# A decoder layer on one core: cross-attention fed by large transfers, with one software-pipelined stream

## The reference

```python
x = x + attn(layernorm(x), ...)                 # linear attention, no softmax
# cross-attention, 16 heads of 8, expanded to 16 features per head
f(t) = concat([exp(t @ fm_w.T + fm_b), exp(-(t @ fm_w.T + fm_b))])   # per head
q = f(layernorm(x)); k = f(ctx); v = f(ctx)
scores = einsum('nqhd,nkhd->nhqk', q, k) / sqrt(128)
out = einsum('nhql,nlhd->nqhd', softmax(scores), v)
x = x + out.reshape(N, S, 256) @ fc_w.T + fc_b
x = x + ffn(layernorm(x), ...)                  # top-1 of 16 experts + a shared expert
```

## Time and profile before

| | |
|---|---|
| median of 3 runs | 655.98 us (653.83 to 665.1) |
| the profiled execution | 653.2 us, of which the span from first to last instruction is 651.4 us |
| PE busy | 464.6 us, 71% of the span, mean granted clock 0.866 |
| DVE, ACT, POOL busy | 341.8, 253.6, 190.8 us |
| phase 3: first score product to last residual addition | 199.8 to 424.5 us |

### The profile page before, as it was taken

The page is one execution under the profiler, slowest core; times in us unless marked ns, Lnnn a source line. Parts: engine busy times, 40 slices in busy tenths (PEclk is TensorE's granted clock), DMA queues, the critical chain, the costliest instruction groups (busy, mean ns, idle before and its releaser), DMA issues.

```text
span 651.4 us, 11782 instructions
## 1 busy us (share of the span) xinstructions
PE 464.6 (71%) x3778; PEld 316.6 (49%) x3778; DVE 341.8 (52%) x969; ACT 253.6 (39%) x578; POOL 190.8 (29%) x223
## 2 busy tenths in 40 slices
PE   0488898677731298888889888868982198887760
PEld 0266566444421166566566665524551155766650
DVE  4577885427686246666665666475820123434343
ACT  0446655377750034444443444536710012323320
POOL 3142231657882000000000000020077400555550
PEclk9999999878885559988985889969997599989995
DMA  5720000016689979999997890000041001566739
GB/s 98 282 95 1 0 0 2 0 42 195 198 144 174 181 89 112 117 105 113 104 112 75 90 97 3 3 1 1 1 145 52 33 0 45 157 194 188 203 95 258
DMA packets 101485, 61.94 MB, mean 95 GB/s; under 512 B 33832, under 2 KB 99656, under 8 KB 101320
## 3 DMA queue, kind: packets, MB, share of 16 engines
q1 hardware_dynamic: 91976, 52.92, 46.7%
q0 software_dynamic: 2560, 5.31, 2.4%
q10 hardware_dynamic: 6912, 3.25, 2.2%
HBM read 40.34 MB, written 20.73 MB: 94 GB/s over the span
## 4 chain that ended last, share of the span: by engine, by line
PE 40%; DVE 15%; SPq 12%; issue 8%; DMA 7%; ACT 7%; another core or an unknown queue 7%; POOL 1%; ACTq 1%; DVEq 0%; POOLq 0%
SPq L473 5%; PE bank L711 4%; PE bank L696 4%; PE bank L1204 3%; DMA kst<-kparts 2%; PE bank L1215 2%; ACT prob L853 2%; PE bank L1214 2%; SPq L629 2%; DMA qst<-mT 2%; PE bank L1263 2%; PE bank L734 2%; PE bank L740 2%; PE bank L666 2%
## 5 line engine op out<-in xcount | busy, mean ns | idle before, releaser
L853 ACT ACTIVATE prob<-bank 77x512 f32<-77x512 f32 x128 | 73.7, 592 | 109.7 <-PE bank L696 109.1
L870 POOL COPY vcur<-vals 77x272 f32 (+1 forms) x32 | 13.2, 416 | 190.5 <-PE bank L711 190.5
L1178 POOL DMA_INDIRECT routed<-t_y,t_no x48 | 45.9, 956 | 75.1 <-DVE t_y L1047 63.9
L778 DVE TENSOR_REDUCE mx<-bank 128x5 f32<-128x385 f32 (+1 forms) x96 | 53.7, 580 | 25.1 <-PE bank L666 23.3
L711 PE MATMUL bank<-prob,vcur 77*17 77x128 f32 x1024 | 57.4, 300 | 12.7 <-ACT prob L853 12.4
L666 PE MATMUL bank<-kst,qst 96*128 96x77 bf16 x512 | 40.7, 224 | 34.2 <-DMA kst<-kparts 28.9
L696 PE MATMUL bank<-qst,kst 99*77 99x128 bf16 x512 | 57.4, 243 | 6.7 <-DMA qst<-mT 6.7
L696 PEld LDWEIGHTS bank<-qst,kst 99*77 99x77 bf16 x512 | 43.8, 132 | 17.1 <-issue 9.4
L825 DVE COPY avs_s<-bank 128x512 f32<-128x512 f32 x32 | 22.1, 692 | 56.7 <-PE bank L711 56.7
L666 PEld LDWEIGHTS bank<-kst,qst 96*128 96x128 bf16 x512 | 31.7, 114 | 37.3 <-DMA kst<-kparts 15.5
L941 DVE TENSOR_TENSOR act<-bank,s_g 128x512 f32<-128x512 f32 x24 | 16.5, 688 | 63.3 <-ACT s_g L1115 49.9
(11 more groups left out here) (178 smaller groups left out, 1071.7 us busy)
## 6 DMA issues: line engine op xcount, KB each, us to landing
qst<-qparts SPq DMA_DIRECT2D x96, 128.0 KB, 5.3
t_w<-in_expert_w SPq DMA_DIRECT2D x48, 192.0 KB
qparts<-qpart SPq DMA_DIRECT2D x16, 384.0 KB, 3.4
kparts<-kpart SPq DMA_DIRECT2D x48, 77.0 KB
kst<-kparts SPq DMA_DIRECT2D x16, 231.0 KB, 7.8
sorted_in<-fill SPq DMA_DIRECT2D x1, 3168.0 KB, 10.4
t_row<-sorted_in ACTq DMA_DIRECT2D x48, 66.0 KB
kst<-kparts SPq DMA_DIRECT2D x16, 154.0 KB, 8.1
```

Of the source, the lines that this page charges most:

```text
L778: v.tensor_reduce(mx[:, n // 3, h0:h1], bank[n % 2][:, 0:(h1 - h0) * KEYS].rearrange("p (h k) -> p h k", k=KEYS), AX.X, ALU.max).then_inc( ...
L853: a.activation(prob[u % 2][:].rearrange("p c t -> p (c t)"), bank[2 + u % 2][0:KEYS], ACT.Exp, scale=SCORE_SCALE).then_inc(s["expd"], 1)
L1178: p.indirect_dma_start(out=routed, out_offset=bass.IndirectOffsetOnAxis(ap=t_no[r][:].bitcast(U32), axis=0), in_=t_y[r][:], in_offset=None ...
```

## The change

- **Layout.** `qparts` and `kparts` are now (group, part, feature, head, token), so that all heads and all tokens of a group lie together in one run for a given part and feature: 16 KB for queries (16 heads x 512 tokens of bf16), 9,856 B for keys. To write so, the feature map's columns are ordered feature outside, head inside; each half of the map holds one sign. A write of parts is one transfer per half for keys too (four a group in place of eight).
- **Loads.** A load is for a group of 4 sequences: `load_q` has three transfers and `load_k` three, and the rows of `qst` and `kst` are numbered with the feature outside and the pairing inside. The pairings that use the same query part are read by one transfer with a repeated source. There are three buffers, each of 4 sequences; the third lies in the arena of phase 2. Groups 0 and 1 are loaded in the middle of phase 2 (from group iterations 2 and 3, and 5 and 6); group 2 after all writes; the others when the buffer's last shifted product is done.
- **One stream.** The steps are written out (no loops in phase 3). The value product stands two sets behind the shifted product (LAG = 2), with three `prob` buffers and two banks for the value sums (4 and 5). `avs` is copied by ACT. Values are read in place, without `vcur`.
- **Shift.** The maxima are negated by the reduction itself. The shift's two transfers are issued by POOL. The bias is added by POOL a sequence at a time.

```diff
-    NBUF = 4
+    NBUF = 3
-        qparts = nc.dram_tensor("qparts", (HEADS, EX, PARTS, TOK), BF16).ap()
-        kparts = nc.dram_tensor("kparts", (PARTS, EX, HEADS, B * KEYS), BF16).ap()
+        qparts = nc.dram_tensor("qparts", (NG, PARTS, EX, HEADS, GT), BF16).ap()
+        kparts = nc.dram_tensor("kparts", (NG, PARTS, EX, HEADS, JK), BF16).ap()
...
+            for g in range(NG):
+                if g < NG - 2:
+                    sp.wait_ge(s["ctxTp"], g + 1)
+                    ctx_load(g + 2, g % 2)
+                if g == 2:
+                    sent(0, 1)
+                    load_q(sp, 0)
+                if g == 3:
+                    load_k(sp, 0)
+                if g == 5:
+                    sent(1, 2)
+                    load_q(sp, 1)
+                if g == 6:
+                    load_k(sp, 1)
+                body(g)
...
                     a.copy(vals[:, bass.ds(g * JP + 2 * jj, 2), :, 0:EX],
-                           bank[5 + jj][0:KEYS].rearrange("p (j h e) -> p j h e", j=2, e=EX)).then_inc(s["v_ready"], 1)
+                           bank[5 + jj][0:KEYS].rearrange("p (j e h) -> p j h e", j=2, e=EX)).then_inc(s["v_ready"], 1)
...
+        def load_q(sp, group):
+            r = group % NBUF
             for at, part, n in Q_RUNS:
-                for i in range(n):
-                    sp.dma_start(qst[r][(at + i) * EX:(at + i + 1) * EX],
-                                 qparts[:, :, part, bass.ds(g * JA * S, JA * S)].rearrange("h e t -> e h t")).then_inc(parts_in[r], 16)
+                same = qparts[group, part].rearrange("e (o h) t -> e o h t", o=1).broadcast_to([EX, n, HEADS, GT])
+                sp.dma_start(qst[r][at * EX:(at + n) * EX], same).then_inc(parts_in[r], 16)
+        def load_k(sp, group):
+            r = group % NBUF
             for at, part, n in K_RUNS:
                 sp.dma_start(kst[r][at * EX:(at + n) * EX],
-                             kparts[part:part + n, :, :, bass.ds(g * JA * KEYS, JA * KEYS)].rearrange("a e h t -> (a e) h t")).then_inc(parts_in[r], 16)
+                             kparts[group, part:part + n].rearrange("a e h t -> e a h t")).then_inc(parts_in[r], 16)
...
         def sp_phase3(sp):
+            all_sent(sp, NG // 2)
+            sp.wait_ge(s["vp"], NG)
+            load_q(sp, 2)
+            load_k(sp, 2)
+            for group in range(3, NG):
+                sp.wait_ge(s["bp"], (group - 2) * (2 * 4 * JA))
+                load_q(sp, group)
+                load_k(sp, group)
...
+            for b in range(JP):
+                for u in range(len(UNITS)):
+                    scores(b, u)
+                if b == 2:
+                    turn_shift(0)
+            for n in range(STEPS):
+                b, u = n // 4, n % 4
+                shifted(n)
+                if n >= LAG:
+                    attend(n - LAG)
+                if u < len(UNITS) and b + JP < B:
+                    scores(b + JP, u)
+                if u == 0 and b % JA == 0 and b // JA + 1 < NA:
+                    turn_shift(b // JA + 1)
+                if u == 1 and b >= 2:
+                    turn_back(b - 2)
+                if u == 2 and b >= 2:
+                    project(b - 2)
+                if u == 3 and b >= 1:
+                    turn_values(b - 1)
...
+        def act_phase3(a):
+            copy_shift(0)
+            for n in range(STEPS):
+                b, u = n // 4, n % 4
+                exponentials(n)
+                if u == 0 and b % JA == 0 and b // JA + 1 < NA:
+                    copy_shift(b // JA + 1)
+                if u == 1 and b >= 1:
+                    copy_values(b - 1)
+                if u == 1 and b >= 2:
+                    copy_back(b - 2)
...
+        def pool_phase3(p):
+            p.wait_ge(s["xn2"], NG)
+            for b in range(JA):
+                add_bias(b)
+            shift(0)
+            all_sent(p, NG // 2)
+            p.wait_ge(s["vp"], NG)
+            p.wait_ge(s["xb2"], JA)
+            p.memset(kst[NBUF - 1][ROWS:SHIFT_ROWS], 1.0).then_inc(s["ones_rows"], 1)
+            p.wait_ge(s["ones_rows"], 1 + NBUF)
+            for g in range(1, NA):
+                shift(g)
                 for j in range(JA):
+                    add_bias(g * JA + j)
```

More of the change, by code:

```diff
@@ new lines, in dve_phase3 @@
+            for b in range(B):
+                for u in range(len(UNITS)):
+                    if b + JP < B:
+                        maxima(b + JP, u)
+                if b >= 2:
+                    add_attention(b - 2)
+                if b >= 1:
+                    divide(b - 1)
+                if b >= 2:
+                    statistics(b - 2)
+                if b % JA == JA - 1 and b + JP < B:
+                    parts((b + JP) // JA)
+            add_attention(B - 2)
+            divide(B - 1)
@@ L1335, in _ @@
             sp_fill(sp)
-            sp_phase2(sp, lambda g: load_parts(sp, g, g))
+            sp_phase2(sp)
             sp_phase3(sp)
```

417 lines of the change are left out of this document (174 added, 243 removed).

## The result

The changed kernel takes 681.04 us (median of 4 runs, 676.52 to 684.50), the kernel before 655.84 us on the same chip (4 runs, 653.83 to 665.10). The ratio is 1.039, 95% interval 1.030 to 1.048: slower, where 8% faster was forecast. The profiled execution took 683.24 us, 30.0 more than that of before, with a granted clock of 0.79 against 0.87. Executions of one kernel scatter by some per cent, and a ratio with an interval leaves out those that were more than 1.5% above the kernel's shortest.

The account below looks back on a forecast made before the run. The prediction took phase 3 as bounded by its stream's start, a PE-bound sequence with some waiting, and the tail. Stream start 206.5 + 165 = 371 us, 53 us sooner, so 653.2 - 53 = 600 us; range 576 to 628.

Parts of the forecast that it names:

- part 5: Clock in the attention: half clock only at the start and one short stretch, 24 us, three sequences of 8.0 us.
- the sum: Phase 3's stream: 3 x 8.0 + 25 x 4.75 = 143, plus 16 and a 5.7 us tail, together 165 us.
- this rival: Clock stays down in the attention: chance 0.12 for more half clock, 613 us; 0.03 for slower, near 695 us if throughout.
- Part 3: Start of phase 3's stream: waits for keys fall away, start at 206.5 us against 228.5, range 203 to 215.
- The rival of POOL's late shift: Attention: the shift takes 8 us beside loads, so 2 us of wait 15 times, 630 us; chance 0.11.
- Part 2: Loads within phase 2: 11 us a group load, making phase 2 2 us longer, range 0 to 6.
- The extreme of 22 us: Group load in phase 2 at the old small-piece rate: 22 us each, adding 31 us.
- Part 4: One attention sequence at full clock: 4.75 us in place of 5.01, the wait for the exponential removed.
- some 0.2 us to spare: DVE's strict order within a sequence: scores arrive just as their bank is free, with some 0.2 us of slack.
- part 1: End of phase 2: POOL's big addition cut into 32, last casts 1.3 us not 11.4, DVE free at 192 not 201.5.
- (b): Theory of the follow-up runs, attention: a shift issued behind a load lands with that load's end.
- (a): Theory of the follow-up runs, phase 2: the loads within it hold it up.

Follow-up runs that it names:

- the late loads: Changed kernel with groups 0 and 1 loaded after phase 2's last writes instead of in its middle; 703.4 us, ratio 1.067 to the kernel before.
- the two paced versions: Changed kernel with group 1 loaded after phase 2, later loads in halves, maxima split early; with one dense product a sequence 623.8 us (1.004), without 621.8 us (0.998).
- best version: Changed kernel with loads of groups 2 to 7 after each sixteen's third set, maxima split early, one dense product a sequence; 591.2 us, ratio 0.964.
- the early split: Edit to the changed kernel, never run alone: DVE takes the maxima apart for the shift right after it has them, ahead of its additions and division.
- Lag: Changed kernel with the value product one set behind the shifted product instead of two; 688.4 us, ratio 1.044.
- order: Changed kernel with PE's order within a sequence put back to that of the kernel before; 685.1 us, ratio 1.121.
- clustering: Changed kernel with a sequence's projection moved from the third set to the fourth, ahead of the next values' turns; 653.3 us, ratio 1.052.
- the paced kernel: Changed kernel with group 1 loaded after phase 2, later loads in halves, maxima split early, no dense product; 621.8 us, ratio 0.998.
- loads at set 3: Changed kernel with loads of groups 2 to 7 issued when the third set of each sixteen is done; alone 610.8 us, ratio 0.992.
- the first eight runs: The first eight follow-up variants, all of the changed kernel; 681.9 to 703.4 us, with the kernel before at 661 us beside them.
- two variants of the old kernel: Kernel before with one dense product a sequence, 613.1 us (0.979); the same with more dense products in its first two load waits, 614.4 us (1.000).

## Why the prediction was wrong

**What failed is part 5, the clock**: "I expect the start and one short stretch: 24 us". Phase 3 ended at 459 us and not at 371; of these 88 us, 13 are the start of the stream and 74 the stream itself. At half clock there were 202 us from 200 us on, some 180 of them in the stream. At 8.1 us that is 22 sequences in place of 3, each 3.3 us above the 4.75 of the sum: 19 x 3.3 = 63 us. The stream from first shifted product to last addition took 239 us, forecast 165; the 74 us are these 63 and most of the later shift waits of 13.8 us. I had this rival, and its price of 3.25 us a sequence was about right (8.1 against 4.75, or 5.07 as measured), but I gave its slow end 3%, since the clock "got up again each time". It did here too, only later: the falls within the stream lasted some 41, 44 and 27 us and the last one to the end of the phase, where in the kernel before they lasted some 3, 3, 27 and 3 us, ahead of one at its very end. The profile had more to say: the earlier trace rows showed PE 97% busy at 0.50 in this very mix. With a busy PE at half clock and no reason seen for its return, "fewer waits" is no argument.

**Part 3, the start**: mis-sized twice. Stream start at 219.8, not 206.5: 7 us for the later end of phase 2, and the rest for the shift. The 3.9 us for the shift's landing would have done for a shift with no load beside it (median 2.2 us), not for one issued behind a load. I wrote that "the next load has the 19 us of a group for its 11" and did not ask what else must land in these us. The rival of POOL's late shift had the symptom, at 8 us of landing, waits of 2 us at 15 places; it was 8.5 us at the first and 11 to 13 at the later ones, and waits at 5 places.

**Part 2**: a group load took 19 us from its first issue to its last landing, not 11 (15.2 us is its last transfer alone). That is 133 GB/s for the 2.52 MB; by the engines' busy time with it alone (67.4% of 303 to 326 us, 15.5 us) it is 163, where the prediction had 230. The extreme of 22 us was nearer than 11. The 11.6 us that I had worked out from the Trainium skill ("SBUF — State Buffer", the DMA port section) was short of the measured time as well. Phase 2 ended 11 us later for the two loads in it, as the late loads showed, where I added 2, with a range to 6. The path is the one that I named, ACT waiting for writes two groups back; I thought its slack would take the excess.

**Part 4** left out a wait: at full clock every second sequence has one of 0.87 us for the split maxima, and the mean is 5.07 us, not 4.75. DVE's split stands behind its additions and division; "some 0.2 us to spare" was asked of the score banks and not of this.

**Right**: large pieces; the waits of 13.4 and 8.1 us for keys gone; L711's waits for exponentials gone; half clock unchanged at 8.1; part 1's mechanism, since the last pair of casts took 1.89 us in place of 11.37; phase 4 unchanged within 5 us; strided values' copies at no visible cost.

**How the loss splits**, as far as runs show. Shown by one edit: (b), with the clock that hangs on it; the ratio went from 1.04 to 0.99 by medians and to 0.97 by the shortest execution, so it is worth some 5%, within a scatter of the same size. Shown by one edit: the dense product shortens the time at half clock, from 202 to 72 us at twice a sequence and from 146 to 95 at once; in the versions that have it a fall within the stream lasted 3 to 14 us. That it pays in time is shown for the kernel before alone (2%). (a) is 11 us; the late loads removed it at a greater cost, and the two paced versions with only group 1 loaded late sent their first shift 3 to 4 us sooner. Not shown: how much of the best version's last 3% is the dense product and how much the early split, which were made together, and the split alone was never run, though PE's waits for it went. By the shortest executions (588.5 and 594.6 us) these 3% are 1%. Open: why a busy PE stays at half clock, and why the stream of before, with the same products, got back so much sooner. Lag, order and clustering were tried and are not it; chance is part of it, for the changed kernel had 202 us in one profiled execution and 160 in another.

## What to carry to other kernels

A small transfer that an engine waits for must be issued ahead of a large load, not behind it: moving the load by three sets, in one edit, was worth some 5%. Price a PE-bound stream at both clock levels, and take the lower one as likely wherever the profile shows a busy PE that stays there; removing waits need not bring the clock back. Count short waits for small operands too: they stood ahead of falls of the clock, and hoisting a small split by a few instructions takes them away. If the clock stays down, try one dense product a sequence, even a useless one, and watch the granted clock and the time separately: twice a sequence gave the clock and lost the time, and once gained 2% in one kernel and nothing in another.

## What the runs showed of the hardware that I had not expected

PE busy 80.00 us of 80 at a clock of 0.51, and 108 of 110 at 0.50. One float32 product of 128x128 by 384 columns a sequence, as the only difference, took the half clock of the paced kernel from 146 to 95 us; with loads at set 3 and the early split besides, the clock was 0.91 over 202 us. A wait of 0.93 us at full clock stood ahead of a fall every 17.1 us, some 3 us after the clock had risen. A 12 KB transfer issued 3.5 to 4.2 us behind the first transfer of a 2.5 MB load took 11.0 to 13.4 us and landed 1 to 4 us before the load's end; issued 0.3 us behind it took 8.7 us, 0.3 us ahead of it 2.1 us, as with no load at all. With three times as many transfers it landed no sooner. And ACT's stall of some 35 us in phase 4 was there in both kernels of the result and in the first eight runs, and absent in the later ones, two variants of the old kernel among them; no run tells why. A small cast took twenty times its usual 0.18 us while POOL filled the third buffer with ones; DVE and POOL of the kernel after, in order of time:

```profile
212.08 4.09 DVE L783 CAST mpart<-mx 128x32 bf16<-128x32 f32 x1
...
211.93 4.20 POOL L895 MEMSET kst<- 3x4928 bf16 x1
```

So one engine holding up the other, as the prediction read it from the earlier trace rows, is there for small operations too, and splitting the big addition was right.
